# Which states' C products GpSimd makes in a selective-scan kernel: the odd ones 1 to 13 in place of the even ones 0 to 12

## The reference, cut to what matters

```
dA = exp(clip(dt * A, -5, 5))
dB = dt * B_t * u_t
state = dA * state + dB + 1e-06
y = sum(state * C_t) + D * u_t          # the sum is over the 16 states
...
y = y * silu(z);  out = y @ out_w.T
```

## Time and profile before

| | |
|---|---|
| median of 3 runs | 2821.62 us (2820.95 to 2825.63) |
| the profiled execution's own time | 2822.5 us |
| its span | 2820.8 us |
| PE busy | 2504.7 us (89%) |
| DVE busy | 2232.6 us (79%) |
| ACT busy | 2028.4 us (72%) |
| POOL busy | 2235.1 us (79%) |
| mean granted PE clock | 0.959 |
| stretch of the chunks, 500 to 900 us: DVE, POOL, PE, ACT busy of 400 us | 382.04, 381.16, 353.81, 348.33 |
| one chunk (gate product L1321 to the next), pos 1, 2 and 3 of one sequence, and pos 0 of the next | 66.47, 66.71, 65.14, 64.50 us |

### The profile page before, as it was taken

One profiled execution on the slowest core, in us unless ns is written; L12 is line 12 of the kernel. 1 busy time (PEld: TensorE's weight loads), 2 busy tenths in 40 slices (PEclk: granted clock), 3 DMA queues, 4 the chain that ended last, 5 costly groups with the idle time before them and its releaser, 6 DMA issues.

```text
span 2820.8 us, 48368 instructions
## 1 busy us (share of the span) xinstructions
PE 2504.7 (89%) x15192; PEld 2193.0 (78%) x15192; DVE 2232.6 (79%) x4907; ACT 2028.4 (72%) x4669; POOL 2235.1 (79%) x1352
## 2 busy tenths in 40 slices
PE   7788898888888888989898988888886899999998
PEld 4677877777777778878787777777775678888887
DVE  2999999999999999999999999999998233333332
ACT  2888888888888888888888888888885223333332
POOL 1999999999999999999999999999995233333333
PEclk9899999999999999999999999999997899999999
DMA  4222222222322222222222223222221488888886
GB/s 178 76 84 84 83 80 82 86 80 82 98 92 82 82 88 91 80 91 84 80 87 81 80 81 108 84 83 83 91 76 46 106 220 204 202 199 201 201 200 153
DMA packets 137333, 307.98 MB, mean 109 GB/s; under 512 B 14960, under 2 KB 79088, under 8 KB 136944
## 3 DMA queue, kind: packets, MB, share of 16 engines
q1 hardware_dynamic: 110288, 268.65, 30.9%
q0 software_dynamic: 26784, 36.20, 6.4%
HBM read 257.04 MB, written 47.75 MB: 108 GB/s over the span
## 4 chain that ended last, share of the span: by engine, by line
PE 38%; DVE 34%; ACT 14%; issue 9%; POOL 1%; DMA 0%; DVEq 0%; POOLq 0%; ACTq 0%; SPq 0%
PE bank L691 13%; DVE bank L1301 13%; PE bank L699 9%; DVE room L1301 8%; DVE room L1310 6%; PE bank L585 6%; ACT room L839 6%; ACT bank L855 5%; PE bank L633 3%; PE bank L649 2%; PE bank L563 2%; PE bank L622 1%; ACT bank L897 1%; PE bank L596 1%; DVE zs L1276 1%
## 5 line engine op out<-in xcount | busy, mean ns | idle before, releaser
L1085 POOL TENSOR_TENSOR room<-dtu,b_all 128x1024 f32<-128x1024 f32 x512 | 1205.3, 2373 | 20.4 <-DVE dtu L1528 13.9
L855 ACT ACTIVATE bank<-room,eps_col 128x512 f32<-128x512 f32 x1024 | 696.1, 683 | 242.1 <-DVE carry L1315 164.0
L839 ACT ACTIVATE room<-room,neg_a 128x256 f32<-128x256 f32 x2048 | 868.8, 499 | 0.8 <-DVE room L1267 0.8
L633 PE MATMUL bank<-ident,room 128*128 128x128 f32 x4096 | 560.1, 284 | 176.2 <-DVE room L1310 89.7
L633 PEld LDWEIGHTS bank<-ident,room 128*128 128x128 f32 x4096 | 486.2, 146 | 233.4 <-DVE room L1310 101.8
L1301 DVE TENSOR_TENSOR_SCAN bank<-room,carry,bank 128x256 f32<-128x256 f32 x864 | 578.1, 734 | 21.1 <-ACT bank L855 20.5
L1074 POOL TENSOR_TENSOR room<-room,c_all 128x1024 f32<-128x1024 f32 x224 | 532.3, 2376 | 47.8 <-issue 28.7
L1215 POOL DMA_INDIRECT out<-room,ids x142 | 221.8, 1562 | 421.5 <-DMA out<-room,ids 203.0
L1301 DVE TENSOR_TENSOR_SCAN room<-room,carry,bank 128x256 f32<-128x256 f32 x672 | 448.1, 726 | 11.2 <-ACT bank L855 10.6
L1390 DVE SCALAR_TENSOR_TENSOR room<-room,bank 128x256 f32<-128x256 f32 (+1 forms) x213 | 89.5, 420 | 409.5 <-ACT room L955 374.7
L585 PE MATMUL bank<-xnT,w_conv 128*128 128x256 f32 x3072 | 405.3, 288 | 7.0 <-ACT xnT L878 5.5
(11 more groups left out here) (169 smaller groups left out, 3012.4 us busy)
## 6 DMA issues: line engine op xcount, KB each, us to landing
b_all<-b_scratch SPq DMA_DIRECT2D x128, 512.0 KB, 4.0
c_all<-b_scratch SPq DMA_DIRECT2D x128, 512.0 KB, 5.2
room<-in_wgu SPq DMA_DIRECT2D x71, 704.0 KB, 5.9
room<-in_wd SPq DMA_DIRECT2D x71, 384.0 KB
room<-x_by_expert SPq DMA_DIRECT2D x71, 260.0 KB
x_in<-in_x SPq DMA_DIRECT2D x32, 256.0 KB, 5.9
x<-in_x SPq DMA_DIRECT2D x32, 256.0 KB, 2.7
out<-x SPq DMA_DIRECT2D x32, 256.0 KB, 4.3
```

Source lines behind the costliest of these rows:

```text
L633: last = mm(tr_bank[k][:, b * P:(b + 1) * P], v[n % VRING][:, b, k * P:(k + 1) * P], ident[:, :], is_transpose=True, start=False, stop=(n ...
L839: last = af(da[n % RING][:, b, :], dt[c.par][:, b, :], ACT.Exp, scale=neg_a[:, b, n:n + 1])
L855: af(v_slot(c, n, h)[:, :], v[n % VRING][:, 2 * h:2 * h + 2, :].rearrange("p b t -> p (b t)"), ACT.Identity, bias=eps_col[:, 0:1]).then_in ...
L1085: nc.gpsimd.tensor_tensor(out=v[n % VRING][:, :, :], in0=dtu[:, :, :], in1=row, op=ALU.mult) \
```

## The change

`BY_POOL` names the states whose product POOL makes. The list keeps its length, so each engine has the same number of products as before; they fall into other slots, against side work that stays where it was. On POOL the product of state n moves with n from slots 1, 3, ..., 13 to slots 2, 4, ..., 14. On ACT `keep_last` moves from even to odd slots. The second hunk adds a wait on DVE in the last chunk but one; what it waits for is an earlier instruction of DVE itself.

```
-BY_POOL = [0, 2, 4, 6, 8, 10, 12]
+BY_POOL = [1, 3, 5, 7, 9, 11, 13]
...
                     step.did(last)
+                    if c.index == CHUNKS - 2:
+                        dve.wait_ge(table_step, 1)
                     vec_e.tensor_copy(base[:, :], o_bank[:, NT * EXPERTS:(NT + 1) * EXPERTS]).then_inc(o_free, 1)
```

## The result

The changed kernel takes 2844.24 us in the median of 4 runs (2842.65 to 2846.31), against 2823.62 us for the kernel before (2820.95 to 2828.43). The ratio is 1.0073, with a 95% interval of 1.0056 to 1.009: **0.7% slower**, just outside the range of 2803 to 2844 us, where no change was forecast. The profiled execution has a span of 2841.7 us, 20.9 more than before.

A forecast was written before the change was run, and what follows sets the result against it. It took DVE's waits for ACT's bank fills, in a loop of PE, ACT and DVE, as the bound. Terms of +0.34 and -0.38 gave -0.04 us a chunk, times 31 = -1.2 us: 2820.4 us, range 2803 to 2844.

The forecast's parts named there:

- What bounds the kernel: DVE, the fullest engine, waits for ACT's bank fills, 35.2 us in 53 waits, in a loop of PE, ACT and DVE.
- The gate in slot 11: DVE's second gate product would newly wait 1.16 us for ACT; slots 10 and 11 take 9.30 us, against 8.14 without it.
- Slots 8 to 10: From slot 8's second half to slot 10's start, slot 9's DVE wait goes: 7.57 us instead of 8.39, 0.82 gained.
- Slots 4 to 8: ACT's fill no longer waits for DVE's product of state 5: -0.38 us a chunk, between 0 and 0.84 by PE's clock.
- POOL's last product: State 13's product, now behind a scatter, delays PE's transposes; costed at 0, up to 0.9 us without cover.
- The sum: Per chunk, 0.34 - 0.38 = -0.04 us, times 31 = -1.2 us: no change, 2820.4 us.
- The rest at nothing: Products moved among slots 0 to 4, later norm statistics in slot 2, the added wait and expert tiles: 0.
- rival 2: Slower: slot 11's gate costs 0.34 us a chunk, slots 4 to 8 give nothing; +10.5, 2832 us; chance 0.20.
- rival 3: Slower: POOL's late product makes PE's down projection up to 0.9 us late each chunk; 27 us, 2847 us; chance 0.13.
- Rival 1: Faster: slow clock always falls on the transposes, ACT starts early every chunk; -0.50 a chunk, 2806 us; chance 0.22.
- rival 4: Slot 11's new wait does not appear because ACT runs far enough ahead; -0.82 stands whole, 2795 us; chance 0.05.
- The slow clock: PE's half-clock stretch always follows its gap at once, by the skill's rule: full 0.84 gained, -0.50 a chunk, 2806 us.

The follow-up runs named there:

- Experiment 4: The changed kernel with POOL's list set to states 1, 3, 5, 7, 8, 10, 12: 2822.92 us, ratio 1.0006 to the kernel before.
- experiment 8: The kernel before, with two of three passes of PE's first convolution put ahead of the transposes of state 15: 2806.86 us, ratio 0.9948.
- experiment 11: The changed kernel with POOL's states 1, 3, 5, 7, 8, 10, 12 and PE's first convolution begun before state 15's transposes: 2818.88 us, ratio 0.9991.
- experiment 12: The kernel before with only the change's second hunk, the added DVE wait in the last chunk but one: 2823.18 us, ratio 1.0009.
- experiment 1: The changed kernel with POOL's first scatter moved behind the product of state 13 and the second weight to slot 15: 2857.55 us, ratio 1.0117.

## Why the prediction was wrong

- **What bounds the kernel:** right as far as tested. Each experiment that gained or lost time did it at a wait of the loop from PE over ACT to DVE.
- **The gate in slot 11:** right. 9.30 us for slots 10 and 11 was forecast for a chunk of position 2, and 9.34 is the mean of that position; that the mean of all is 9.28 is luck. A wait of 1.16 us was forecast, 1.2 measured (38.6 us in 32). The cost was still under-counted, because the 8.14 us it was set against holds for positions 1 and 2 alone. The mean of before is 7.99, since these slots take 7.66 us in position 0 (the first chunk of a sequence scans faster) and 8.01 in position 3 (no carry copies). The term is +1.29, not +1.16.
- **Slots 8 to 10:** right in kind, too large. -0.82 forecast, -0.61 measured. In chunks of position 2 it is -0.84, so here too the one chunk stood for all; and DVE, now early, waits for PE's routing matmul (7.0 us in 18 waits).
- **Slots 4 to 8, the step that failed.** -0.38 was forecast, 0.00 measured. Its part on PE's clock came true: the down projections took 2.92 us instead of 3.61, one slow one of 30 instead of 18. Two things ate that. *POOL's last product*, which I costed at 0, lets the projection start over 0.6 us late in 11 of 30 chunks, 1.9 us in several of position 1. The forecast worked out one kind of chunk, position 2, and there it had POOL right: 62.7 us after the chunk's start for the end of that product, 62.7 measured. In position 0 the product ends only 3.2 us before DVE is through, and three sets of transposes at the slow clock take 5.2 us; the forecast had two sets at that clock. And the fill behind the next product was overlooked: making state 5 POOL's freed ACT's fill of slot 5 (the forecast's text says slot 4), but made state 6 DVE's, and the fill of slot 6 waits for it. ACT's uT was 0.21 us early in the mean (24.44 to 24.23) and dt was not early at all. That the mean is 0.00 hides the positions: in 0 and 3 dt did gain 0.38 us, position 1 lost 0.63 and position 2 lost 0.09. How the 0.38 splits between the two causes is open. Experiment 4, with the same first half and no late projection, has dt 0.12 us early, so the larger part is missing without the late product too. The fill's wait is shown by experiments 8 and 11; no kernel gave state 6 alone back to POOL.
- **The sum:** -0.04 was forecast, +0.67 measured: -0.61 + 1.29 + 0.00, and -0.01 behind slot 12. Of the miss of 0.71 us, 0.38 is the step that failed, and the one chunk that stood for all is the rest (0.21 and 0.13).
- **The rest at nothing:** right. The norm statistics did make POOL wait, 48.7 us in 22 waits at L1090 (35.4 in 2 before). Experiment 4 has nearly the same waits (48.1 in 20) and is as fast as before, so they cost nothing that shows. The added wait was right at 0 within 0.2% (experiment 12).
- **The rivals.** The result lies between rival 2 (+10.5 us, nothing gained ahead of slot 8) and rival 3 (+27 us, the late product). Both of their mechanisms are there: the gain is absent, in part because of the late product. Rival 1 and rival 4 did not happen. Rival 3's sign, L699 late behind DVE's last gated product, is seen in 11 of 30 chunks.
- **The slow clock:** the rule of the Trainium skill, page "TensorE: Matmul & The Clock Gate", section "Why this matters for your kernels", that gaps drop PE to half clock, agrees with the clock of 0.50 behind the 4.19 us gap; the sum by it (2806 us) does not, as it left out DVE's product of state 6 and the late product of state 13. That the slow stretch follows the gap at once was the forecast's reading of the rule, and in the kernel before it didn't always: behind the 2.25 us gap that ended at 1250.47 the transposes of state 15 took 1.09 us, at full clock, and the down projection from 1251.96 on 4.52 us. PE's row from the kernel before:

```profile
1250.47 1.09 PE L633 MATMUL bank<-ident,room 128*128 128x128 f32 x8 [2.25 <-DVE room L1310]
```

What is left open: how much of experiment 1's 13 us is the slow clock and how much the order of PE's work in that stretch. No kernel kept PE's clock up without also moving work.

## What to carry to other kernels

Moving which of two engines does an operation, with equal totals, moves who frees a buffer and when: follow the waiting engine through every slot that changes sides, not only the one that improves. When a loop runs over several kinds of chunk, work the sum out for each kind; a timeline of one gave two terms 0.13 and 0.21 us off, which is some 10 us together over 31 chunks. When an engine must wait anyway, ask what it does right behind the wait and at which clock, and put independent work into the gap: that alone made the kernel before 0.5% faster (2806.9 us), better than any list of states tried here. But look first where the gap is: in the changed kernel the same edit put the work behind the gap, and gave nothing.

## What the runs showed of the hardware

The place of a gap matters, and not only its length. Experiment 1 moved PE's gap from before the transposes of state 13 to before those of state 15. PE's waits for the operands of transposes, POOL's and DVE's together, were 175.5 us (68.4 and 107.1), against 167.0 in the changed kernel (148.8 and 18.2), 8.5 more. The down projections close behind the gap took 4.05 us in the mean instead of 2.92, with a granted clock of 0.50 in the one shown, and the kernel took 13 us more. In the changed kernel the transposes behind the gap pay for the slow clock, and have the time in the 19 of 30 chunks whose projection is not late.
